# Layer two of a block in one PSUM group of 128 columns, and one z operation on VectorE

## The reference

```python
router_probs = softmax(xt @ Wr + br)
gates = max(router_probs); idx = argmax(router_probs)
xn = layernorm(xt) * ln_g + ln_b
h = relu(xn @ W1[idx] + b1[idx])          # 128 -> 512
y = (h @ W2[idx] + b2[idx]) * gates       # 512 -> 128
x = layernorm(x + y)
```

## Time and profile before

| | |
|---|---|
| median of 3 runs | 201.93 us (200.13 to 201.94) |
| the profiled execution | 202.25 us, of which the span of instructions is 200.5 us |
| mean granted clock of TensorE | 0.908 of 2.4 GHz |
| busy share of the span | PE 74%, DVE 80%, ACT 74%, POOL 57% |
| blocks of the second stage | first product of layer two at 111.8 us, the last block's at 187.5 us |

### The profile page before, as it was taken

One profiled execution on the slowest core, in us unless ns is written; L12 is line 12 of the kernel. 1 busy time (PEld: TensorE's weight loads), 2 busy tenths in 40 slices (PEclk: granted clock), 3 DMA queues, 4 the chain that ended last, 5 costly groups with the idle time before them and its releaser, 6 DMA issues.

```text
span 200.5 us, 5489 instructions
## 1 busy us (share of the span) xinstructions
PE 147.8 (74%) x1446; PEld 118.1 (59%) x1446; DVE 161.1 (80%) x819; ACT 148.1 (74%) x448; POOL 114.3 (57%) x200
## 2 busy tenths in 40 slices
PE   0068979988997795922369878998998997999400
PEld 0015736857566474821316767987888996888200
DVE  2455287999998869699698899999999999799900
ACT  2358979997975696527645887999999999898520
POOL 4323140508789765634469215768677687578650
PEclk9999999999999998585556999999999999999955
DMA  5997184000101101101342212223222222110000
GB/s 131 346 394 261 26 273 159 3 0 15 40 26 35 42 29 41 54 15 40 77 126 83 56 30 55 66 71 76 65 75 64 66 64 69 53 54 19 28 9 0
DMA packets 16415, 15.74 MB, mean 79 GB/s; under 512 B 2810, under 2 KB 13142, under 8 KB 16386
## 3 DMA queue, kind: packets, MB, share of 16 engines
q1 hardware_dynamic: 14034, 11.10, 19.0%
q0 software_dynamic: 2272, 4.27, 6.4%
q10 hardware_dynamic: 80, 0.03, 0.1%
HBM read 10.52 MB, written 5.33 MB: 79 GB/s over the span
## 4 chain that ended last, share of the span: by engine, by line
PE 43%; DVE 33%; issue 8%; ACT 6%; DMA 3%; ACTq 2%; POOLq 1%; SPq 1%; POOL 0%; DVEq 0%
PE bank L473 7%; DVE hl L1239 6%; PE bank L592 6%; PE bank L430 5%; PE bank L445 4%; DMA XN<-in_attn_embeddings 3%; DVE z L1248 3%; PE bank L502 3%; PE bank L580 3%; PE bank L576 2%; PE bank L578 2%; DVE zpart L1244 2%; PE bank L579 2%; PE bank L595 2%; DVE bn L1252 2%
## 5 line engine op out<-in xcount | busy, mean ns | idle before, releaser
L418 POOL DMA_INDIRECT out<-OUT,tok x39 | 40.5, 1039 | 26.5 <-issue 25.0
L383 POOL DMA_INDIRECT rows<-R,place x32 | 31.8, 994 | 18.0 <-DVE place L919 9.4
L592 PE MATMUL bank<-W2hl,hh 128*128 x156 | 32.6, 274 | 7.0 <-issue 3.2
L576 PE MATMUL bank<-sel,bias 96*128 96x128 bf16 x156 | 34.6, 222 | 0.0
L578 PE MATMUL bank<-xh,W1h 128*128 128x128 f16 x156 | 34.2, 219 | 0.0
L580 PE MATMUL bank<-xh,W1l 128*128 128x128 f16 x156 | 34.1, 218 | 0.0
L579 PE MATMUL bank<-xl,W1h 128*128 128x128 f16 x156 | 34.0, 218 | 0.0
L1239 DVE SCALAR_TENSOR_TENSOR hl<-bank,hh 128x512 f16<-128x512 f32 x39 | 26.9, 690 | 3.5 <-ACT hh L746 2.6
L595 PE MATMUL bank<-W2hl,hl 128*128 x156 | 27.9, 219 | 0.0
L746 ACT ACTIVATE hh<-bank 128x512 f16<-128x512 f32 x39 | 23.1, 593 | 6.1 <-PE bank L580 5.8
L359 POOL TENSOR_TENSOR rmag<-guarded,minus_half 128x4 f32<-128x4 f32 x8 | 8.2, 1022 | 27.0 <-ACT guarded L615 27.0
(11 more groups left out here) (197 smaller groups left out, 459.3 us busy)
## 6 DMA issues: line engine op xcount, KB each, us to landing
XR<-rows SPq DMA_DIRECT2D x39, 66.0 KB
W<-in_ffn_W SPq DMA_DIRECT2D x1, 2048.0 KB, 11.0
X<-in_attn_embeddings SPq DMA_DIRECT2D x2, 512.0 KB, 8.6
X<-in_attn_embeddings SPq DMA_DIRECT2D x1, 768.0 KB
out<-OUT,tok POOLq DMA_INDIRECT x39
rows<-padt SPq DMA_DIRECT2D x9, 66.0 KB
XN<-in_attn_embeddings SPq DMA_DIRECT2D x2, 256.0 KB, 7.9
rows<-R,place POOLq DMA_INDIRECT x32
```

The lines of the kernel that those rows point to most:

```text
L383: pool.indirect_dma_start(out=rows[:, :], out_offset=bass.IndirectOffsetOnAxis(ap=place[u][:, k:k + 1], axis=0), in_=R[u][:, k, :], in_off ...
L418: pool.indirect_dma_start(out=out[:, :], out_offset=bass.IndirectOffsetOnAxis(ap=tok[k][:, 0:1], axis=0), in_=OUT[k][:, :], in_offset=None ...
L576: pe.matmul(h, bias3[:, c * P:(c + 1) * P], sel, start=True, stop=False)
L592: pe.matmul(y[:, 0:2 * D], hh[k][:, c * P:(c + 1) * P], w, start=c == 0, stop=False)
```

## The change

Layer two of a block goes into one group of 128 columns. The product of 256 columns becomes two of 128, both with hh as the stationary operand, one with the high and one with the low half of the weight, and both add to columns 0 to 127. So there are twelve products and the bias, thirteen instead of nine. The operation z0 with its tile and its semaphore goes, and z is one operation from the bank and the row; the reload of a row buffer waits for z instead of z0.

```diff
@@ SP
             def load(count, k):
-                after(sp, every["z0"], blocks(count(-1), k))
+                after(sp, every["z"], blocks(count(-1), k))
@@ PE, b_y
                 for c in range(FC):
-                    w, wh = W2hl[:, bass.ds(e, 1), c, :], W2hl[:, bass.ds(e, 1), c, 0:D]
-                    pe.matmul(y[:, 0:2 * D], hh[k][:, c * P:(c + 1) * P], w, start=c == 0, stop=False)
+                    wh, wl = (W2hl[:, bass.ds(e, 1), c, part * D:(part + 1) * D] for part in range(2))
+                    pe.matmul(y[:, 0:D], hh[k][:, c * P:(c + 1) * P], wh, start=c == 0, stop=False)
+                    pe.matmul(y[:, 0:D], hh[k][:, c * P:(c + 1) * P], wl, start=False, stop=False)
                     if c == 0:
                         pe.matmul(y[:, 0:D], sel16[:, count(0) * UN + k:count(0) * UN + k + 1].to_broadcast([96, P]), bias3[:, FF:FF + D], start=False, stop=False)
                     m = pe.matmul(y[:, 0:D], hl[k][:, c * P:(c + 1) * P], wh, start=False, stop=c == FC - 1)
@@ DVE
-            def b_z0(count, k):
+            def b_z(count, k):
                 dve.wait_ge(every["y_ps"], blocks(count(0), k))
-                stt(z0[k][:, :], bank[5 + k % 2][:, 0:D], cg[k][:, :], XR[k][:, 0:D], ALU.mult, ALU.add).then_inc(every["z0"], 1)
-
-            def b_z(count, k):
-                dve.wait_ge(every["z0"], blocks(count(0), k))
-                stt(z[k][:, :], bank[5 + k % 2][:, D:2 * D], cg[k][:, :], z0[k][:, :], ALU.mult, ALU.add).then_inc(every["z"], 1)
+                stt(z[k][:, :], bank[5 + k % 2][:, 0:D], cg[k][:, :], XR[k][:, 0:D], ALU.mult, ALU.add).then_inc(every["z"], 1)
@@
-            steps([(1, b_hl), (-1, b_mv), (0, b_z0), (-2, b_rec), (0, b_z), (-2, b_shift), (0, b_bn), (0, b_table), (4, b_xl), (4, b_split)])
+            steps([(1, b_hl), (-1, b_mv), (-2, b_rec), (0, b_z), (-2, b_shift), (0, b_bn), (0, b_table), (4, b_xl), (4, b_split)])
```

More of the change, by code:

```diff
@@ L191, in build @@
         hl = [sb(f"hl{i}", [P, FF], F16) for i in range(UN)]
-        z0 = [sb(f"zpart{i}", [P, D]) for i in range(UN)]
         z = [sb(f"z{i}", [P, D]) for i in range(UN)]
@@ L209, in build @@
         padded = sem("padded")
-        every = {n: sem("every_" + n) for n in "token xs xh xl hl z xT_ps xt h_ps hh y_ps z0 bn mv sd rec shift out".split()}
+        every = {n: sem("every_" + n) for n in "token xs xh xl hl z xT_ps xt h_ps hh y_ps bn mv sd rec shift out".split()}
         seen = sem("seen")
```

## The result

The changed kernel takes 208.76 us (median of 4 runs, 208.24 to 209.51) against 201.76 for the kernel before on the same chip: 1.037 times as long, interval 1.031 to 1.043, or 7.0 us more between the medians. The forecast was 204.7 us and its range ended at 206.4. The profiled execution took 208.79 us with a span of 207.0.

A forecast was written before the change was run, and what follows sets the result against it. ScalarE bound the kernel before at 1.88 us per block; the sequencer would bind at 1.94. Block 38 starting 2.5 us later plus 0.3 for a late product made +2.8 on 201.93: 204.7 us, range 200.3 to 206.4.

The forecast's parts named there:

- (b): TensorE's sequencer: eight layer-two steps take 1.00 us, the block's sum is 1.94 us, above ScalarE's 1.88.
- (c): Loads of block numbers on TensorE's sequencer, no longer absorbed: 1.1 us at block 4, about 3.3 us for later ones.
- (a): TensorE's products: thirteen take 0.74 us against 0.72, the block 1.76 us, under ScalarE's 1.88; cost nil.
- (d): VectorE without zpart: gains 1.2 us in the first stretch, 0.3 and 0.3 at the end, nothing from 126 to 180.
- The sign named against it: In the profile after, z starting later than 0.2 us behind mv would show the VectorE term wrong.
- (e): Row buffer reload waits for z, about 0.15 us later than zpart; row wanted over 5 us on: nil.
- the late product: At block 30 hh stood idle for a late product; 0 to 0.5 us would return, 0.3 added.
- (1): Rival: single-product steps are short or the queue keeps the sequencer ahead; only VectorE's gain remains, 200.1 us; chance 0.20.
- (2): Rival: single-product sequencer steps of 0.110 to 0.115 us, sum 1.88 to 1.90; 202 to 203 us; chance 0.16.
- (3): Rival: waits or fetching 12 more instructions per block cost the sequencer 0.03 us more each period; 206 us; chance 0.07.

The follow-up runs named there:

- z alone: The kernel before with z in one operation, its nine products and four register operations kept, low weight half left out of the output: 199.22 us, ratio 0.991.
- the fewer-products kernel: The changed kernel without eight of its thirty products per block, all sixteen register operations kept: 209.75 us, ratio 1.036.
- the one with twelve operations: The changed kernel with layer one's low weights fixed at expert 0, so twelve register operations per block: 204.69 us, ratio 1.007; once more 204.87 us.

## Why the prediction was wrong

The mechanism was right, and the term that failed is **(b)**, the sequencer's sum: it said 1.94 us per block, and the runs show 2.09. (c) was mis-sized too, by less and the other way.

- (a) Products cost nothing. Right: with the low half at a fixed address all thirteen run in a kernel at 198.4 us with ScalarE as the bound. The rate of 0.057 us per product held too: there, thirteen take 150.94 - 150.20 = 0.74 us. By the Trainium skill's 81 ns ("TensorE: Matmul & The Clock Gate", "Back-to-back issue gap") they would take 1.05 us, an estimate, so the trace does not agree.
- (b) "Now layer two has eight steps, 1.00 us, and the sum is 1.94 us." The plain steps are exactly that: 8 × 0.124 + 4 × 0.124 + 4 × 0.1125 = 1.94, and a step with one product between is 0.124, as with two or three. What was left out is the longer step after every eighth register operation. Sixteen operations meet it twice a block: 2 × 0.072 = 0.14 to 0.15, and the period is 2.09. Over 38 blocks this is 5.7 us, more than the whole miss of 4.1. It stood in the trace of the kernel before; the earlier trace rows look at three steps and one pair, and a stretch that short can easily hold none of the long ones, and these held none. I took a step for the rate.
- (c) Too big. From block 8 on it had 3.3 us for three loads, and the traces show 2.64; ahead of block 4 it had 1.1, and they show 0.42. What it said of the kernel before was wrong as well: the earlier trace rows give the idle time ahead of hl, 1.85 us, and not how late the blocks come, which is 2.54. The change adds 0.45 us at the loads, where the term had 1.45 and 1.1.
- (d) Right in size: 1.8 us by z alone. Not right in that nothing comes from 126 to 180 us, since 1.0 us of what the trace gains lies at the late blocks there. The sign named against it did show: z starts 0.32 us behind mv (163.66 - 163.34), not 0.21. But there VectorE has slack, and the reciprocal ahead of z starts only at 163.58. In the first stretch of the kernel with z alone, where it matters, it is 0.14 (116.37 to 116.51). In the changed kernel nothing of it is left before block 8, as the sum said.
- (e) Right: in the changed kernel ScalarE never stands idle ahead of xs for its row (before, 0.6 us in two places).
- The sum, put right: +2.8, + 5.7 for the eighth steps, - 1.3 for the loads, - 0.3 for the late product that did not return (30 × 2.09 + 2.64 = 65.3, and 65.25 was measured), makes +6.9; measured +7.0. That it closes so well is in part luck: the first eight blocks took 17.50 us, where these terms give 17.1, and what lies behind the last block's first product took 12.8 instead of 13.0.

Of the rivals, (1) was out as soon as the step with one product came out at 0.124, and (2) with it. (3) named the direction, "waits, or the fetching of more instructions", but priced it at 0.03 us per block without a row behind the number, where 0.15 was to be read; and the fewer-products kernel and the kernel before show that it is register operations that count, not instructions or time. The forecast's own bounds, 0.122 to 0.129 on twelve steps of 38 blocks, are - 1.4 and + 1.8 us around 204.7, so its 203.7 to 205.8 was narrower than what it was said to come from. With the range's upper end at 206.4 it trusted a step of 0.125 to within 4 ns, when what was uncertain was whether steps were all alike.

Of what the profile was to show: 312 register operations, steps of 0.124, ScalarE idle ahead of hh and released by L579, and busy under 15.4 us, VectorE under 14, pairs with gaps. These hold. A period near 1.94 does not. At the loads ahead of blocks 12, 20 and 28 hl comes 0.8, 0.8 and 1.4 us later than a plain period would bring it, which is near the 0.9 to 1.3 that was said.

## What to carry to other kernels

Before splitting a product whose operand's address sits in a register, count the register operations per iteration on TensorE's sequencer and compare steps × 0.124 us, plus 0.07 us for every eighth (the figures of this kernel), with the period of the engine that binds; columns and products may be free while addresses are not. Take a rate over at least one whole iteration and look for steps that differ, since a short window shows the step and not the rate. An engine whose sequencer lags looks busy in the profile (here TensorE with 15.3 of 16 us), so ask what a fixed address would do: one kernel with the address fixed separates the two in a single run.

## What the runs showed of the hardware

- One register operation of TensorE's sequencer is recorded with 46 ns, but the next one comes 124 ns later, with one, two or three products between; behind an ALU_OP it is 112 to 113.
- After eight of them a step is 15 to 190 ns longer, 61 to 85 ns in the mean, in every kernel here that has them. The distance is eight with 22 or 30 products per block, and with 1.04 or 1.32 us between (changed kernel, kernel before). What causes it no run shows.
- A load of eight numbers into registers is recorded with 0.59 to 0.78 us, the last one, of seven numbers, with 1.07 to 1.15. Four of them lengthen the time from the first hl to the last by 2.6 us in the kernel before, 3.1 in the changed kernel and 3.8 in the one with twelve operations.
